# Second attention: where the second copies of the high parts of K and Q are made

## The reference, cut to what matters

```
keys = jnp.einsum('bse,neh->bsnh', residual, W_key) + Bias_key
queries = jnp.einsum('bse,neh->bsnh', residual, W_query) + Bias_query
values = jnp.einsum('bse,neh->bsnh', residual, W_values) + Bias_values
scores = jnp.einsum('bknh,bqnh->bnqk', keys, queries) / jnp.sqrt(H)
scores = jnp.where(q_idx < k_idx, EPS, scores)
probs = jax.nn.softmax(scores, axis=3)
weighted = jnp.einsum('bnqk,bknh->bqnh', probs, values)
out = jnp.einsum('bqnh,nhe->bqe', weighted, W_output) + Bias_output
```

## Time and profile before

| | |
|---|---|
| median of 3 runs | 2333.4 us (2332.91 to 2341.03) |
| profiled execution | 2326.48 us, its span 2324.7 us |
| TensorE busy | 2015.7 us, 87% of the span |
| VectorE busy | 1415.8 us, 61% |
| ScalarE busy | 1001.3 us, 43% |
| GpSimd busy | 568.2 us, 24% |
| mean granted TensorE clock | 0.912 of full speed |

### The profile page before, as it was taken

How to read it: one execution, slowest core, us unless ns; L and a number is a source line. 1 busy time by engine, 2 the same in 40 slices (tenths; PEclk the granted TensorE clock), 3 DMA queues, 4 the chain that set the end, 5 groups by cost and what they waited for, 6 DMA issues and landing times.

```text
span 2324.7 us, 31839 instructions
## 1 busy us (share of the span) xinstructions
PE 2015.7 (87%) x10080; PEld 1164.4 (50%) x10080; DVE 1415.8 (61%) x2400; ACT 1001.3 (43%) x1422; POOL 568.2 (24%) x543
## 2 busy tenths in 40 slices
PE   5899999996977999997768999999869789998975
PEld 3444444443764555545644444444348545555554
DVE  5577787866335666652366777778562466666422
ACT  2444444441224566652225444444313336666411
POOL 0000000000002686785120000000000046687831
PEclk6899999998896999998959999999979879999987
DMA  2256565577000000000513565555760000000015
GB/s 89 60 148 149 142 149 140 139 168 236 3 1 9 6 5 5 1 1 28 153 34 88 142 148 147 150 143 143 173 197 1 1 10 10 1 5 1 1 52 152
DMA packets 84846, 187.99 MB, mean 81 GB/s; under 512 B 17697, under 2 KB 46754, under 8 KB 83106
## 3 DMA queue, kind: packets, MB, share of 16 engines
q1 hardware_dynamic: 83650, 183.76, 30.1%
q0 software_dynamic: 1024, 2.10, 0.3%
HBM read 178.47 MB, written 8.91 MB: 81 GB/s over the span
## 4 chain that ended last, share of the span: by engine, by line
PE 58%; DVE 15%; ACT 10%; issue 10%; POOL 3%; DMA 3%; SPq 1%; DVEq 0%; ACTq 0%; POOLq 0%
PE PS L792 6%; PE PS L762 5%; PE PS L747 4%; PE PS L902 4%; PE PS L730 4%; PE PS L942 3%; PE PS L752 3%; PE PS L962 3%; DVE EE L1854 3%; DVE mx L1825 3%; PE PS L945 3%; PE PS L1133 3%; ACT EE L1455 2%; PE PS L857 2%; POOL Esum L2320 2%
## 5 line engine op out<-in xcount | busy, mean ns | idle before, releaser
L1825 DVE TENSOR_REDUCE mx<-PS 128x8 f32<-128x512 f32 x512 | 330.0, 685 | 196.2 <-PE PS L730 190.4
L1455 ACT ACTIVATE EE<-PS 128x1024 f32<-128x1024 f32 x256 | 262.1, 1024 | 265.3 <-PE PS L752 264.4
L2320 POOL TENSOR_TENSOR Esum<-Esum,EE 128x512 f32<-128x512 f32 (+3 forms) x320 | 336.1, 1078 | 15.5 <-POOL Esum L2320 10.1
L1854 DVE TENSOR_TENSOR EE<-EE,V 128x1024 f32<-128x1024 f32 x256 | 309.9, 1216 | 40.3 <-DMA V<-weight_rows 39.8
L792 PE MATMUL PS<-EE,Vlater 128*64 128x512 f32 x1024 | 275.4, 617 | 28.9 <-DVE EE L1854 28.2
L1956 DVE TENSOR_REDUCE mrow<-PS 128x1 f32<-128x512 f32 (+3 forms) x384 | 205.9, 552 | 131.3 <-PE PS L905 104.3
L2274 POOL TENSOR_TENSOR U<-xn,norm_aff 128x1024 f32<-128x1024 f32 x2 | 4.7, 2358 | 1107.7 <-DVE QA L2245 1107.7
L747 PE MATMUL PS<-QA,KA 128*128 128x512 f32 x512 | 201.7, 476 | 10.6 <-ACT EE L1455 9.3
L1532 ACT ACTIVATE EE<-PS 128x1024 f32<-128x1024 f32 (+2 forms) x192 | 139.4, 738 | 120.9 <-PE PS L945 118.3
L730 PE MATMUL PS<-KA,QA 128*128 128x512 f32 x512 | 182.5, 436 | 8.2 <-DVE KB L1809 3.4
L752 PE MATMUL PS<-QB,KB 80*128 80x512 f32 x512 | 165.2, 404 | 0.0
(11 more groups left out here) (304 smaller groups left out, 3359.7 us busy)
## 6 DMA issues: line engine op xcount, KB each, us to landing
V<-weight_rows SPq DMA_DIRECT2D x512, 256.0 KB, 4.4
EE<-in_w SPq DMA_DIRECT2D x48, 192.0 KB, 2.7
V<-in_Wg SPq DMA_DIRECT2D x4, 1024.0 KB, 6.6
EE<-in_Wu SPq DMA_DIRECT2D x4, 1024.0 KB, 11.6
EE<-in_Wd SPq DMA_DIRECT2D x4, 1024.0 KB, 13.5
sorted_out<-U SPq DMA_DIRECT2D x12, 256.0 KB, 3.1
wo<-in_wo SPq DMA_DIRECT2D x5, 512.0 KB, 16.2
wq_s<-in_wq SPq DMA_DIRECT2D x17, 128.0 KB, 7.7
```

What stands on the lines that cost most here:

```text
L1455: act.activation(EE[i % 2][:, t, :], banks(0), ACT.Exp, scale=QSCALE).then_inc(s["p2_exp"], 1)
L1825: dve.tensor_reduce(mx[:, t, half * 8:half * 8 + 8], banks(5 + x % 2, BANK).rearrange("p (c k) -> p c k", c=8), AX, ALU.max).then_inc(s["p ...
L1854: dve.tensor_tensor(EE[i % 2][:, t, :], EE[i % 2][:, t, :], weight_ring[a % 2][:, odd, :], ALU.mult).then_inc(p3_mul, 1)
L2320: ins = pool.tensor_tensor(Esum[:, h, lo:hi], Esum[:, h, lo:hi], e_tile(t)[:, h, lo - t * P:hi - t * P], ALU.add)
```

## The change

Only the making of the second copies changes.

- K: `high_k` writes S1 alone. A new function `second_k(p)` copies K high from S1 to S2, for both heads, over all 1024 columns, from SBUF. It is called once per pair, in mid-pair behind the inverse (for the next pair), and once in the prologue for pair 0.
- Q, first half (half 0): still two copies by ACT, in the other order (the upper partitions first).
- Q, second half (half 1): ACT writes only partitions 0 to 63. DVE copies them to partitions 64 to 127, from SBUF, just ahead of its subtraction.

```diff
@@ high_k
-                        act.activation(S2[h][p % 2][0:HD, cols], src, ACT.Identity, bias=bias)
                         act.activation(S1[h][p % 2][0:HD, cols], src, ACT.Identity, bias=bias).then_inc(s["hi_out"], 1)
@@ high_q
-                        act.activation(M1[h][p % 2][0:HD, cols], src, ACT.Identity, bias=bias)
-                        act.activation(M1[h][p % 2][HD:P, cols], src, ACT.Identity, bias=bias).then_inc(s["hi_out"], 1)
+                        if half == 0:
+                            act.activation(M1[h][p % 2][HD:P, cols], src, ACT.Identity, bias=bias)
+                        act.activation(M1[h][p % 2][0:HD, cols], src, ACT.Identity, bias=bias).then_inc(s["hi_out"], 1)
+
+                def second_k(p):
+
+                    act.wait_ge(s["hi_out"], 8 * (n0 + p) + 8)
+                    for h in range(2):
+                        act.activation(S2[h][p % 2][0:HD, :], S1[h][p % 2][0:HD, :], ACT.Copy)
@@ pair, on ACT
                     if prev:
                         inverse(p - 1)
+                    if follows:
+                        second_k(p + 1)
                     exponents(p, 3, 0)
@@ prologue, on ACT
                     high_k(p, half)
                     high_q(p, half)
+                second_k(0)
                 row_b(0)
@@ low_q, on DVE
                         dve.wait_ge(s["hi_out"], 8 * n + 4 * half + 2 + h + 1)
+                        if half == 1:
+                            dve.tensor_copy(M1[h][p % 2][HD:P, cols], M1[h][p % 2][0:HD, cols])
                         dve.scalar_tensor_tensor(out=M2[h][p % 2][0:HD, cols],
```

## The result

The changed kernel takes 2302.0 us in the median (2295.11 to 2305.2, 4 runs), the kernel before 2335.13 us in the same series (2332.91 to 2341.03, 4 runs). The ratio is 0.985, its 95% interval 0.983 to 0.988: 33 us faster. Run a second time as an experiment, the same kernel gave 0.9825 (0.980 to 0.985). The forecast was 2289, with a range of 2270 to 2320. The profiled executions are 27.3 us apart by their spans, 2324.7 and 2297.4.

The account below looks back on a forecast made before the run. TensorE was taken to bound the kernel, with border waits and the low clock following them. Terms of -19.8 us without the clock and -24.5 for the clock gave -44.3, a 2289 us median, range 2270 to 2320.

Parts of the forecast that it names:

- The border: Between pairs, the chain ACT, DVE, PE shortens by 1.1 us at six borders with a predecessor: -6.6 per batch.
- Clock at the interior borders: Behind interior borders, shorter PE waits remove the low clock at five of six: -12.2 us per batch.
- late part, -3.9 per batch: Late in six pairs, ACT skips K's second copies; DVE's 0.66 wait goes and PE's falls from 0.91 to 0.25.
- The middle, +7.2 per batch: Behind the inverse, K's copies delay tile 3's exponent; PE waits, 1.2 us in each of pairs 1 to 6.
- The first border, -2.1: At pair 0's border, with POOL idle, the chain shortens fully: -2.1 us per batch.
- The prologue, -4.5: In the three K and Q blocks before the first maxima, fewer ACT operations save 4.5 us per batch.
- the first (the clock still falls): Rival: PE's thin work and remaining border wait keep the low clock; 2314 us, chance 0.17.
- The second (the copies meet POOL): Rival: DVE's border copies wait for POOL each time, the border wait stays 1.1 to 1.3; 2327 us, chance 0.10.
- The third (the middle becomes the border): Rival: ACT's copies delay mid-pair beyond 1.5 us, so PE runs slow there in pairs 1 to 6; 2349 us, chance 0.05.

Follow-up runs that it names:

- the K part alone: The change with only its K part, Q's second copies by ScalarE from PSUM as before, against the kernel before: 2297.04 us, 0.983.
- the Q part alone: The change with only its Q part, K's second copies from PSUM on the border as before, against the kernel before: 2331.35 us, 0.9965.
- the two kernels with VectorE's copies whose turn came 0.9 us sooner: The changed kernel with one-step row maxima: 2304.87 us, 0.985 to 0.988 excluded here, ratio 0.986; with K's copies behind tile 4's exponents too: 2301.46 us, 0.985.

## Why the prediction came out as it did

- *The border.* Right. Forecast 1.1 per border, ends 0.7 and 1.46; PE's wait fell from 1.46 to between 0.12 and 0.24, 1.3 per border and 7.7 per batch. The 0.35 I took for the copy's waiting for POOL was too much.
- *Clock at the interior borders.* Right, and shown by putting the wait back: ten low pieces per batch went, 14.7 us, where I had counted on 12.2.
- *The step that failed: late part, -3.9 per batch.* PE's wait for the maximum fell as said, 0.91 to 0.28. But the term was carried to the sum without asking what is late next. In pairs 1, 2, 4 and 5 the turn's wait rose by 0.5, because DVE's mask copy, reached sooner, takes 0.99 instead of 0.49 beside POOL's normalisation. L1976 behind it is held as long as before, 0.94. A row of such holding was in my hands, and I used it for the copy of Q alone. Measured for six pairs: -1.9 (pair 0, where PE doesn't wait at the turn, keeps its 0.65).
- *The middle, +7.2 per batch.* The mechanism was right in pairs 1 to 5, and the wait of 0.93 lay between my ends: taking it away gave 5.0 for the 6.0 forecast. Pair 6 was mis-sized. It has no late part, its waits of 0.94, 0.85 and 1.47 and a low stretch follow one another, and it cost 5.25 where I had 1.2. In the K part alone pair 6 has the first two of these waits without a low stretch, in both batches, and lasts 37.96: so 2.2 of the 5.25 hang on the low clock and the longer wait at the turn. I had priced one place and multiplied by six. Together 10.3.
- *The first border, -2.1.* The chain was shorter (waits of 2.51 and 1.47 became 0.65 and 1.19), but the low clock there lasted 10.2 us instead of 6.8, which takes back 1.47.
- *The prologue, -4.5.* From its first row on ACT to the first turn it became 4.6 shorter in batch 0 and 4.75 in batch 1; the 4.8 used below for batch 0 holds 0.2 that lies ahead of it.

With these the sum for batch 0 up to the last turn is -4.8 - 7.7 (six borders) - 2.1 + 1.5 - 1.9 + 10.3 - 14.7 = -19.4, and the profile has 4.8 + 14.6 = 19.4. Behind the last turn, which I had at nothing, the second attention is shorter by another 1.7 in batch 0 and 0.5 in batch 1 of this profile. From its first row on ACT to the end of its output projection it became 20.9 us faster in batch 0 and 19.7 in batch 1, 40.6 in all, against 44.3 forecast. That this is so near is luck: in batch 0 the middle cost 3.1 more than I had, the late part gave 2.0 and the first border 1.5 less, while the clock and the interior borders gave 3.6 more and the stretch behind the last turn 1.7.

The profiled executions moved by 27.3, 13.3 less than that: this lies outside the changed code, in the mixture stretch of batch 1 (9.4, its two forms), the expert block of batch 0 (3.3) and smaller pieces. The medians, over more executions, moved by 33. No term of mine allowed for that; the range was wide enough for it.

Of the rivals, the first (the clock still falls) did not occur. The second (the copies meet POOL) did not occur here, but it did in others: with the Q part alone in pairs 2, 4 and 6 (copy 0.91, wait 1.47), and in the two kernels with VectorE's copies whose turn came 0.9 us sooner. The third (the middle becomes the border) occurred in pair 6 only. I had set its limit at a wait of 1.5 us. That number was the wrong kind: at the border 0.92 to 1.08 was mostly enough, in the middle 0.93 did nothing in pairs 1 to 5, and 2.18 brought the low clock in six of twelve pairs. So what else PE does around the wait counts too, though no run varied that alone. I had judged 0.76 at the border safe since 0.91 in the late part did no harm; the conclusion held only because the wait became 0.24. The Trainium skill (TensorE: Matmul & The Clock Gate, "What's actually happening") has the monitor run free of the program; that equal waits had unequal effects, 1.52 with and without a low stretch in one profile, agrees.

## What to carry to other kernels

Where a shorter chain hands its result to an operation that another engine can hold, the gain is not the time saved but the time until that engine's instruction ends: look at the next such operation before booking it, or replace it by one that can't be held, as the single reduction here. Here that paid only once K's copies stood later and VectorE's copies were off the border (2282.6 us against 2304.9 alone). Freed work should be put where its engine idles, read from the timeline and for every kind of pair: one pair in six paid as much as the others together. Compare kernels by stretches of the changed code when the clock elsewhere can move the total by 9 us, and expect that an edit worth 1 us at one place shifts the next place against an engine that did not move.

## What was not expected of the hardware

- A TensorE wait of about 1 us at a thin place brought the lower clock 15 times of 18, one of 0.93 in dense work never in pairs 1 to 5.
- ACT copies of 64x1024 from SBUF take 1.04 us, no less than 128x1024.
- A DVE reduction of 48 columns took 205 ns at most in all 16 cases, 14 of them beside POOL's work; a two-input operation over 16 columns took 941 in the median.
- A DVE mask copy of 128x256 took 0.49 to 0.51 us where it met only the end of a POOL instruction, and 0.98 to 0.99 where it met more of one.
- A stretch of 86 to 99 us takes about 9 us more or less between executions whose code up to there is the same, with 50 to 55 us at the low clock or 32 to 37.
